# Thirteen result buffers, a later combine of the first half, and the positive part of the keys on VectorE

## The chip, the cores and the metric

The kernel runs on one core of a Trainium2 chip. Five engines work side by side, each on its own queue of instructions: TensorE (PE, with PEld for its weight loads), VectorE (DVE), ScalarE (ACT), GpSimd (POOL) and SyncE (SP, which here only issues transfers). They meet through semaphores. The metric is the device time of one execution in microseconds (us), the median of several runs.

## The reference

Two transformer layers in float32 over 2 x 2048 tokens of 128 channels. Layer 0 adds a Hyena attention (a projection, a convolution over three tokens, two long convolutions by FFT) and a mixture of 8 experts with 4 chosen, plus a shared expert. Layer 1, in which the whole change lies, is this:

```
xn = layernorm(x)
q, k = elu(xn @ wq + bq) + 1, elu(xn @ wk + bk) + 1;   v = xn @ wv + bv     # 16 heads of 8
kv = sum over n of k[n] v[n];   out = (q @ kv) / (q . sum k + 1e-6) @ wo + bo
scores[e] = norm(xn @ W_A[e]);   two best of 8 experts, weights by softmax
y[e] = W_down[e] (silu(W_B[e] W_A[e] xn) * W_up[e] xn)
x = x + out + sum over the two chosen experts of weight * y
```

elu(t) + 1 is computed as max(t, 0) + exp(-max(-t, 0)).

## The kernel before

The last two thirds of the time are one loop over 90 slots, written out by hand once for each engine; what an engine does in a slot, and in which order, is the order of the `if`s in its loop. An engine never passes an instruction that waits.

Slots 0 to 47 are eight chunks of 512 tokens, six slots each. In each slot TensorE makes one piece of the layer-0 experts (`gate0`, `up0_step`, `down0_step`), ScalarE its silu (L1174), VectorE the product (L1622) and GpSimd a weighting (L893). Behind that, at fixed distances from a chunk's end, comes layer 1 for that chunk: `due(slot, at)` gives the chunk whose end lies `at` slots back. Normalised tokens are turned, and then keys and values are multiplied in steps 7, 8, 10, 11 (`keys_values`), two tiles of 128 tokens to a bank; VectorE adds their bias in steps 9 and 12 (`key_bias`, L1605); ScalarE does all of `key_features` for both halves in step 13, and the exp of the queries (`query_exp`, L1148); VectorE adds both parts in step 14 (`key_sum`, L1693); TensorE sums keys times values in steps 15 and 16 (`key_value_sum`, L2079). `key_features` is, for each half,

```
nc.scalar.activation(KEX[:, j % 3], k, ACT.Relu, scale=-1.0).then_inc(k_neg, 1)        # L1091
act.wait_ge(k_neg, j + 1)
nc.scalar.activation(k, k, ACT.Relu)                                                    # L1093
nc.scalar.activation(KEX[:, j % 3], KEX[:, j % 3], ACT.Exp, scale=-1.0).then_inc(k_exp, 1)  # L1094
```

and exp needs another activation table than the silu, so a table load stands before the first exp of a block and before the silu after it. The steps of the last two chunks reach into the pair stage: steps 10 and 13 of chunk 6 are pair slots 0 and 3, those of chunk 7 are pair slots 6 and 9.

Slots 52 to 87 are the pair stage: pair slot i = slot - 52, 0 to 35. The tokens have been scattered by expert into rows in HBM (`scatter`, L863, one indirect transfer for 128 rows); there are at most 71 blocks of 128 rows, taken two at a time as 36 pairs. In slot i TensorE turns the rows of pair i+1 (L2099), makes the gate and up products of pair i (`gate_up`, three passes of split floats a block), turns the products of pair i-1 (L2128), and makes the down products of pair i-2 (L2143). Then one step of the attention of a chunk: denominators and numerators twice (L2163), turn (L2169), output product (L2174); this has a period of six slots for two interleaved halves. ScalarE copies rows_hi (L1101), takes the silu of pair i (L1108), copies the turned products of pair i-1 (L1115) and weights the results of pair i-2 into a result buffer (`result_rows`, L1125). VectorE computes rows_lo of pair i+1 (L1635), an attention step, the product of pair i (L1643) and its destinations (L1652 to L1657). The ranks of the last quarter of the router (L1499 to L1512) fall in pair slots 8 and 9; they free the roots on GpSimd (L850).

A result buffer holds one pair; there are YBUFS = 9, and `result_rows(i)` waits until the scatters of pair i - YBUFS have landed. GpSimd scatters the buffers to `result_rows` in HBM (`results`, L878). `shares()` lays down how many scatters GpSimd issues in each slot: PER_SLOT = 3, expert rows first, results with what is left, except that results which a buffer will need are forced. By it slot 16 has three rows and one forced result, slot 17 one row and two results, slots 18 to 33 three results each, slots 34 and 35 two each, and the rest follows behind the loop. GpSimd starts a slot's scatters when the gate products of that slot are done.

The combine brings results back in token order. SyncE's queue carries row loads (L729), and ahead of the row load of pair RESULTS_BEFORE = 34 the four loads of the first half of the tokens (`load_results(0)`, L741, 512 KB each), which wait until the scatters of pairs 0 to 23 (48 blocks) have landed. VectorE adds the first half from slot BACK_AT = 30 on, BACK_STEP = 2 tiles (one call of `combine`, L1665 and L1666) a slot. After the last scatter has landed come `load_results(1)`, the combine of the second half, and the stores.

Of the kernel before, what the change touches and what calls it, by code (L numbers as in the profile page):

```python
# [78 lines left out]
YBUFS = 9  # L79
# [11 lines left out]
BACK_AT, BACK_STEP = 30, 2  # L91
RESULTS_BEFORE = 34
# [9 lines left out]
COUNT_AT = (16, 16, 17, 14)  # L102
RANK_AT = ((13, 14, 15),) * 3 + ((12, 13, 13),)
# [19 lines left out]
def hyena_moe_program(nc, x, w_inT, conv_rows, peT, w1T, b1, w2b, fdec, fbias, w_outT, b_out,  # L123
# [8 lines left out]
    with ctx:  # L132
# [204 lines left out]
        YB = view(rW + 2560, YBUFS, 2, D)  # L337
        KTHF = view(rW + 2560 + YBUFS * 2 * D, RING, 2)
        DEST = view(rW + 2560 + YBUFS * 2 * D + 16, NP, 2).bitcast(I32)
        WROW = view(rW + 2560 + YBUFS * 2 * D + 16 + 2 * NP, RING, 2)  # L340
        KTHW = view(rW + 2560 + YBUFS * 2 * D + 32 + 2 * NP, RING, 2)
        assert 2560 + YBUFS * 2 * D + 48 + 2 * NP <= 5120 and 2 * RING <= 16
# [56 lines left out]
        first_x = sem("first_x")  # L399
        res_mm = sem("res_mm")  # L400
        res_out = sem("res_out")
        bout_in = sem("bout_in")
# [48 lines left out]
        up_hi = sem("up_hi")  # L451
        up_lo = sem("up_lo")
# [90 lines left out]

        def odd_due(s, at):

            c = due(s, at)
            return c // 2 if c is not None and c % 2 else None
# [47 lines left out]

        def last_use(end, n):

            return end - 1 - (end - 1 - n) % YBUFS
# [29 lines left out]
        def _(sp):  # L628
            sp.dma_start(X[:, 0:TPC, :], x[:, 0:TPC, :]).then_inc(first_x, 16)
# [29 lines left out]
            sp.wait_ge(st_wexp, 32)  # L659
# [7 lines left out]
            sp.wait_ge(pool_set, 2)  # L667
# [97 lines left out]
        def _(pool):  # L765
# [50 lines left out]
            for q in range(2 * NJ):  # L816
                if q == NJ:
# [5 lines left out]
                    ins.then_inc(bout_in, 1)  # L823
# [13 lines left out]
            def up_lo_part(n):  # L837

                if n == 0:
                    pool.wait_ge(up_hi, 1)  # L840
                es = slice(2 * n, 2 * n + 2)
                nc.gpsimd.tensor_tensor(out=GUL[:, es, F1W:2 * F1W], in0=UP1[:, es, :],
                                        in1=GUH[:, es, F1W:2 * F1W].bitcast(F32), op=ALU.subtract).then_inc(up_lo, 1)
# [28 lines left out]
            def results(m):  # L872

                for i, n in placed[stored[0]:stored[0] + m]:
                    if n == 0:
# [4 lines left out]
                        in_=YB[:, i % YBUFS, n, :], in_offset=None).then_inc(st_rows[i % YBUFS], 16)  # L880
                stored[0] += m

            for slot in range(SLOTS):
# [13 lines left out]
                if slot == UP_LO_AT + W_PARTS:  # L897
                    pool.wait_ge(split_hi, 3)
                    nc.gpsimd.tensor_tensor(out=WAL[:, :, :], in0=WA1, in1=WAH[:, :, :].bitcast(F32),
                                            op=ALU.subtract).then_inc(split_lo, 1)  # L900
                if slot == UP_LO_AT + W_PARTS + 1:
                    pool.wait_ge(split_hi, 4)
# [23 lines left out]
        def _(act):  # L926
# [124 lines left out]
            def prepare(slot):  # L1051

                if slot == UP_HI_AT:
                    act.wait_ge(ld_w1, N_W1)
                    nc.scalar.activation(GUH[:, :, F1W:2 * F1W], UP1, ACT.Copy).then_inc(up_hi, 1)
# [29 lines left out]
            def key_features(j):  # L1085
# [32 lines left out]
            def result_rows(i):  # L1118
# [5 lines left out]
                for n in range(blocks(i)):  # L1124
                    ins = nc.scalar.activation(YB[:, i % YBUFS, n, :], PS[6][:, P * n:P * (n + 1)], ACT.Copy,  # L1125
# [24 lines left out]
            for slot in range(SLOTS):  # L1150
# [53 lines left out]
        def _(dve):  # L1204
# [73 lines left out]
            def statistics(n):  # L1278
                first, last = PIECES[n]
                dve.wait_ge(ld_x[first // 8] if n else first_x, 16)  # L1280
# [149 lines left out]
            def residual(j):  # L1430

                dve.wait_ge(down_mm, N0 * (j + 1))
                if j == 0:
                    dve.wait_ge(bout_in, 1)
# [164 lines left out]
            def key_bias(j):  # L1599
                dve.wait_ge(kv_mm, j + 1)  # L1600
                if j == 0:
                    dve.wait_ge(pool_set, 3)
# [86 lines left out]
            def key_sum(j):  # L1689
# [3 lines left out]
                nc.vector.tensor_tensor(out=k, in0=k, in1=KEX[:, j % 3], op=ALU.add).then_inc(k_sum, 1)  # L1693
# [15 lines left out]
            for slot in range(SLOTS):  # L1709
# [6 lines left out]
                for h in range(2):  # L1716
                    c = due(slot, 9 + 3 * h)
                    if c is not None:
                        key_bias(2 * c + h)
# [15 lines left out]
                c = due(slot, 14)  # L1735
                if c is not None:
# [36 lines left out]
        def _(pe):  # L1773
# [242 lines left out]
            def turn_normed(c):  # L2016
# [11 lines left out]
            def keys_values(n):  # L2028
# [3 lines left out]
                if n == 0:  # L2032
                    pe.wait_ge(split_lo, 4)
# [15 lines left out]
            def expert_gates(n):  # L2049
                if n:  # L2050
                    pe.wait_ge(sq_in, n)
                else:
                    pe.wait_ge(split_lo, 3)
# [48 lines left out]
            def gate_up(i):  # L2102

                if i == 0:
# [3 lines left out]
                    pe.wait_ge(up_lo, W_PARTS)  # L2108
# [195 lines left out]
```

## Time and profile before

| | us |
|---|---|
| median of 3 runs | 621.71 (619.81 to 622.02) |
| profiled execution, its own time | 618.25 |
| its span, first to last instruction | 616.4 |
| PE busy | 557.1 (90%) |
| DVE busy | 433.7 (70%) |
| ACT busy | 314.3 (51%) |
| POOL busy | 297.4 (48%) |
| mean granted TensorE clock | 0.986 of full speed |

Busy time is a sum over the span and says little of a single stage. A row of a timeline gives the start, the duration, the engine, the line and the form of an instruction, and in brackets the time for which its engine stood idle before it and what ended that. "issue" is time in which the engine waited for nothing that the profile shows. The words "arena" and "banks" stand for all of the program's on-chip memory and for the accumulators of TensorE.

### The profile page before, as it was taken

To read this page: it belongs to the slowest core of one execution; us is meant where nothing else is said; L and a number is where in the kernel's file an instruction comes from. 1 tells how busy PE (TensorE), PEld (TensorE's weight loads), DVE (VectorE), ACT (ScalarE), POOL (GpSimd) and SP (SyncE) were. 2 spreads that over 40 slices of the span, in tenths; PEclk is the share of its full clock that TensorE was granted. 3 is DMA by queue.
4 is the path that set the end of the run, shared out by engine and by line. 5 is a ranking of instruction groups with operands and counts; after the bars stand their busy time and mean duration, and the time that the engine had idled before them with its cause. 6 is when DMAs were issued, how large, how long until landed. Compare 5 with 4: busy or idle time off the path is not lost.

```text
span 616.4 us, 10602 instructions
## 1 busy us (share of the span) xinstructions
PE 557.1 (90%) x3218; PEld 463.2 (75%) x3218; DVE 433.7 (70%) x1153; ACT 314.3 (51%) x625; POOL 297.4 (48%) x269
## 2 busy tenths in 40 slices
PE   6999999999989898999999999998889787999970
PEld 3879986576778676788888888876667676788870
DVE  6868998909931596335565998998878895566673
ACT  3560336764423444144456764765675854456550
POOL 4720030005561355147332446887735777577770
PEclk9999999999999999999999999999899999999995
DMA  6460031310040530323323223212322232323626
GB/s 206 155 256 18 2 136 27 77 44 2 1 138 0 178 118 1 94 70 89 88 81 85 56 79 94 86 42 85 92 57 64 61 103 84 88 83 89 228 82 230
DMA packets 48525, 54.94 MB, mean 89 GB/s; under 512 B 7045, under 2 KB 40390, under 8 KB 47415
## 3 DMA queue, kind: packets, MB, share of 16 engines
q1 hardware_dynamic: 43686, 42.99, 22.4%
q0 software_dynamic: 4320, 8.99, 4.2%
q10 hardware_dynamic: 466, 2.31, 1.7%
q8 instruction: 28, 0.46, 0.3%
q14 instruction: 25, 0.20, 0.1%
HBM read 36.22 MB, written 15.94 MB: 85 GB/s over the span
## 4 chain that ended last, share of the span: by engine, by line
PE 29%; DVE 11%; issue 8%; POOL 7%; ACT 7%; DMA 3%; SPq 0%; POOLq 0%; ACTq 0%; DVEq 0%
PE banks L1784 4%; PE banks L1786 3%; PE banks L1785 3%; PE banks L1992 3%; PE banks L2143 3%; PE banks L1906 2%; DMA arena<-result_rows 2%; POOL arena L893 2%; POOL result_rows L878 2%; PE banks L1898 2%; DMA result_rows<-arena 1%; PE banks L2128 1%; POOL expert_rows L863 1%; PE banks L1919 1%; PE banks L1920 1%
## 5 line engine op out<-in xcount | busy, mean ns | idle before, releaser
L878 POOL DMA_INDIRECT result_rows<-arena x71 | 69.1, 973 | 27.9 <-issue 16.6
L827 POOL TENSOR_TENSOR arena<-arena 128x512 f32<-128x512 f32 x32 | 40.8, 1274 | 86.2 <-DVE arena L1468 86.2
L863 POOL DMA_INDIRECT expert_rows<-arena x64 | 63.2, 988 | 30.9 <-issue 15.9
L893 POOL TENSOR_TENSOR arena<-arena 128x512 f32<-128x512 f32 x32 | 42.3, 1321 | 65.0 <-DVE arena L1622 64.9
L1622 DVE TENSOR_TENSOR arena<-banks,arena 128x512 f32<-128x512 f32 x48 | 33.0, 688 | 42.5 <-PE banks L1786 33.5
L1992 PEld LDWEIGHTS banks<-arena 128*128 128x128 f32 x384 | 48.8, 191 | 7.5 <-POOL arena L893 3.5
L1992 PE MATMUL banks<-arena 128*128 128x128 f32 x384 | 51.6, 277 | 2.5 <-POOL arena L893 1.5
L1898 PE MATMUL banks<-arena 128*128 128x512 f32 x96 | 50.5, 608 | 2.4 <-DVE arena L1468 1.1
L1906 PEld LDWEIGHTS banks<-arena 128*128 128x128 f32 x256 | 33.0, 191 | 19.0 <-POOL arena L827 14.4
L1174 ACT ACTIVATE arena<-banks 128x512 f32<-128x512 f32 x48 | 28.8, 599 | 36.2 <-PE banks L1786 31.7
L994 ACT ACTIVATE arena<-banks 128x512 f32<-128x512 f32 x48 | 28.7, 597 | 32.5 <-PE banks L1874 32.5
L2143 PE MATMUL banks<-arena 128*128 x284 | 38.4, 278 | 4.2 <-ACT arena L1125 3.8
L1023 ACT ACTIVATE arena<-banks 128x512 f32<-128x512 f32 x32 | 19.1, 597 | 39.4 <-PE banks L1906 39.4
L2143 PEld LDWEIGHTS banks<-arena 128*128 128x128 f32 x284 | 34.5, 192 | 5.8 <-issue 5.7
L1466 DVE TENSOR_TENSOR arena<-banks,arena 128x512 f32<-128x512 f32 x32 | 22.1, 692 | 23.7 <-PE banks L1898 22.1
L1906 PE MATMUL banks<-arena 128*128 128x128 f32 x256 | 34.4, 277 | 4.0 <-POOL arena L827 4.0
L1475 DVE TENSOR_TENSOR arena<-banks,arena 128x512 f32<-128x512 f32 x16 | 11.1, 692 | 34.5 <-PE banks L1920 34.5
L1784 PE MATMUL banks<-gate_up_weights_hi,rows_hi 128*128 x71 | 31.7, 446 | 3.6 <-DVE arena L1643 3.6
L1784 PE MATMUL banks<-projection_hi,xnt_hi 128*128 128x384 f32 (+1 forms) x92 | 33.4, 363 | 0.4 <-DVE xnt_lo L1274 0.4
L1643 DVE TENSOR_TENSOR arena<-banks,arena 128x512 f32<-128x512 f32 (+1 forms) x36 | 24.5, 679 | 13.0 <-ACT arena L1108 12.8
L1125 ACT ACTIVATE arena<-banks,arena 128x128 f32<-128x128 f32 x71 | 22.3, 365 | 21.4 <-DMA result_rows<-arena 12.2
L1082 ACT ACTIVATE arena<-banks 128x512 f32<-128x512 f32 x32 | 19.1, 596 | 26.0 <-PE banks L1786 14.1
(277 smaller groups left out, 1625.0 us busy)
## 6 DMA issues: line engine op xcount, KB each, us to landing
arena<-expert_weights SPq DMA_DIRECT2D x64, 128.0 KB, 3.3
arena<-expert_rows SPq DMA_DIRECT2D x71, 66.0 KB, 1.8
arena<-result_rows SPq DMA_DIRECT2D x8, 512.0 KB, 6.1
arena<-in_x SPq DMA_DIRECT2D x7, 512.0 KB, 7.1
arena<-in_dft_f SPq DMA_DIRECT2D x1, 2048.0 KB, 9.9
normed_hi<-xnt_hi SPq DMA_DIRECT2D x1, 2048.0 KB, 6.3
normed_lo<-xnt_lo SPq DMA_DIRECT2D x1, 2048.0 KB, 10.8
arena<-in_dft_i SPq DMA_DIRECT2D x1, 2048.0 KB, 7.7
```

Of the source, the lines that this page charges most:

```text
L827: nc.gpsimd.tensor_tensor(out=T1[:, q % 3, :], in0=T1[:, q % 3, :], in1=T2[:, q % 2, :], op=ALU.add).then_inc(y_in, 1)
L863: pool.indirect_dma_start(out=xrows, out_offset=bass.IndirectOffsetOnAxis(ap=SLOT[:, k, t:t + 1], axis=0), in_=XNF[:, t, :], in_offset=Non ...
L878: pool.indirect_dma_start(out=yrows, out_offset=bass.IndirectOffsetOnAxis(ap=DEST[:, i, n:n + 1], axis=0), in_=YB[:, i % YBUFS, n, :], in_ ...
L893: nc.gpsimd.tensor_tensor(out=AM0[slot % 2], in0=AM0[slot % 2], in1=WB0[:, m, :], op=ALU.mult).then_inc(weighted, 1)
L994: nc.scalar.activation(spread_rows(n % NI), bank(spread_bank(n % NI), 2, NGR, 4), ACT.Copy)\
L1174: nc.scalar.activation(SG0, PS[0], ACT.Silu).then_inc(silu_done, 1)
L1622: nc.vector.tensor_tensor(out=AM0[n % 2], in0=PS[1], in1=SG0, op=ALU.mult).then_inc(mult_done, 1)
L1784: mm(o, lh, rh, start=start, stop=False, skip_group_check=True)
L1898: mm(PS[2 + J % 2], TURNF, ZT[:, J % 2, :], start=True, stop=True).then_inc(d_mm, 1)
L1906: ins = mm(PS[6 + q % 2][:, P * n:P * (n + 1)], T1[:, q % 3, P * n:P * (n + 1)], TURNI, start=True, stop=True)
L1992: ins = mm(PS[2][:, D * t:D * (t + 1)], AM0[n % 2][:, P * t:P * (t + 1)], DW0[:, m, :], start=False, stop=(m == N0 - 1), skip_group_check= ...
L2143: ins = mm(PS[6][:, P * s:P * (s + 1)], AMT[:, i % 2, 2 * s + f, :], DN_FLAT[:, at], start=(f == 0), stop=(f == 1), skip_group_check=True)
```

## The change

The number of result buffers goes from 9 to 13. The first nine stay where they were; the other four lie in the region of the gated weights' staging, which is free by then. `shares()` and the waits follow from YBUFS, so the forced result of slot 16 goes, and slot 34 gets three results. The four loads of the first half stand ahead of the row load of pair 35 where they stood ahead of that of pair 34, and the combine of the first half starts in slot 32 with four tiles a slot where it started in slot 30 with two.

The positive part of the keys is no longer taken on ScalarE; VectorE's key sum takes it in the same instruction, max(k, 0) + exp part. The negative part of each half is taken one slot after its bias (steps 10 and 13), the exps of both halves stay in step 13.

Four semaphores make room for the four new buffers: `first_x` counts on `st_wexp`, `bout_in` on `pool_set`, `up_hi` on `split_hi` and `up_lo` on `split_lo`, with the numbers that are waited for raised accordingly. The steps of the key work are read from tables now, with the numbers that they had for all but the negative parts.

```diff
-YBUFS = 9
+YBUFS = 13
+Y_LOW = 9
-BACK_AT, BACK_STEP = 30, 2
-RESULTS_BEFORE = 34
+BACK_AT, BACK_STEP = 32, 4
+RESULTS_BEFORE = 35
+KEYS_AT = ((7, 8, 10, 11),) * NCH
+KEY_BIAS_AT = ((9, 12),) * NCH
+KEY_NEG_AT = ((10, 13),) * NCH
+KEY_EXP_AT = (13,) * NCH
+KEY_SUMMED_AT = (14,) * NCH
+KEY_VALUE_AT = ((15, 16),) * NCH
...
-        YB = view(rW + 2560, YBUFS, 2, D)
+        YB_LOW = view(rW + 2560, Y_LOW, 2, D)
+        YB_HIGH = view(rG + 2048, YBUFS - Y_LOW, 2, D)
...
+        def parts_due(s, table):
+
+            return [(c, n) for c in range(NCH) for n, at in enumerate(table[c]) if s == N0 * (c + 1) + at]
+        def result_buffer(i, n):
+
+            b = i % YBUFS
+            return YB_LOW[:, b, n, :] if b < Y_LOW else YB_HIGH[:, b - Y_LOW, n, :]
...
-            sp.dma_start(X[:, 0:TPC, :], x[:, 0:TPC, :]).then_inc(first_x, 16)
+            sp.dma_start(X[:, 0:TPC, :], x[:, 0:TPC, :]).then_inc(st_wexp, 16)
-            sp.wait_ge(st_wexp, 32)
+            sp.wait_ge(st_wexp, 48)
...
-                    pool.wait_ge(up_hi, 1)
+                    pool.wait_ge(split_hi, 3)
...
-            def key_features(j):
+            def key_negative(j):
                 act.wait_ge(kv_bias, j + 1)
                 if j >= 3:
                     act.wait_ge(kvs_mm, 2 * (j - 2))
                 k = KVS[:, j % 3, :, 0:P]
                 nc.scalar.activation(KEX[:, j % 3], k, ACT.Relu, scale=-1.0).then_inc(k_neg, 1)
+
+            def key_exp(j):
+
                 act.wait_ge(k_neg, j + 1)
-                nc.scalar.activation(k, k, ACT.Relu)
                 nc.scalar.activation(KEX[:, j % 3], KEX[:, j % 3], ACT.Exp, scale=-1.0).then_inc(k_exp, 1)
...
-                    ins = nc.scalar.activation(YB[:, i % YBUFS, n, :], PS[6][:, P * n:P * (n + 1)], ACT.Copy,
+                    ins = nc.scalar.activation(result_buffer(i, n), PS[6][:, P * n:P * (n + 1)], ACT.Copy,
...
-                c = due(slot, 13)
-                if c is not None:
-                    key_features(2 * c)
-                    key_features(2 * c + 1)
+                for c, h in parts_due(slot, KEY_NEG_AT):
+                    key_negative(2 * c + h)
+                for c in chunks_due(slot, KEY_EXP_AT):
+                    key_exp(2 * c)
+                    key_exp(2 * c + 1)
                     query_exp(c)
...
-                nc.vector.tensor_tensor(out=k, in0=k, in1=KEX[:, j % 3], op=ALU.add).then_inc(k_sum, 1)
+                nc.vector.scalar_tensor_tensor(out=k, in0=k, scalar=0.0, in1=KEX[:, j % 3], op0=ALU.max,
+                                               op1=ALU.add).then_inc(k_sum, 1)
...
-                    pe.wait_ge(up_lo, W_PARTS)
+                    pe.wait_ge(split_lo, 2 + W_PARTS)
```

## Rows read from the trace of the kernel before

**Rows 1.** Waits, 450 us on: who waited for whom, total, times, longest
```profile
ACT arena L1125 <- DMA result_rows<-arena: 12.2, 4, 5.3
```

**Rows 2.** ScalarE's timeline: start, us, line, form, [idle before, releaser]
```profile
521.25 0.63 ACT L1125 ACTIVATE arena<-banks,arena 128x128 f32<-128x128 f32 x2 [5.26 <-DMA result_rows<-arena]
...
598.45 0.37 ACT L1125 ACTIVATE arena<-banks,arena 128x128 f32<-128x128 f32 x1 [1.00 <-PE banks L2143]
```

**Rows 3.** GpSimd's timeline, pair stage
```profile
488.13 2.93 POOL L850 TENSOR_TENSOR arena<-arena 128x16 f32<-128x16 f32 x1 [1.74 <-DVE arena L1512]
...
491.50 1.19 POOL L878 DMA_INDIRECT result_rows<-arena  x1 [0.17 <-issue]
...
518.92 0.95 POOL L878 DMA_INDIRECT result_rows<-arena  x1 [0.30 <-issue]
...
596.32 1.17 POOL L878 DMA_INDIRECT result_rows<-arena  x1 [0.30 <-issue]
...
601.58 0.95 POOL L878 DMA_INDIRECT result_rows<-arena  x1 [0.30 <-issue]
```

**Rows 4.** TensorE's timeline: gate products of pairs 17,21,23,25,27,31,33
```profile
516.64 0.49 PE L1784 MATMUL banks<-gate_up_weights_hi,rows_hi 128*128 x1
...
537.75 0.48 PE L1784 MATMUL banks<-gate_up_weights_hi,rows_hi 128*128 x1
...
545.49 0.49 PE L1784 MATMUL banks<-gate_up_weights_hi,rows_hi 128*128 x1
...
553.29 0.48 PE L1784 MATMUL banks<-gate_up_weights_hi,rows_hi 128*128 x1
...
560.69 0.47 PE L1784 MATMUL banks<-gate_up_weights_hi,rows_hi 128*128 x1
...
576.08 0.48 PE L1784 MATMUL banks<-gate_up_weights_hi,rows_hi 128*128 x1
...
585.04 0.48 PE L1784 MATMUL banks<-gate_up_weights_hi,rows_hi 128*128 x1
```

**Rows 5.** The page's part 5: busy, mean ns, idle before, releaser
```profile
L878 POOL DMA_INDIRECT result_rows<-arena x71 | 69.1, 973 | 27.9 <-issue 16.6
```

**Rows 6.** ScalarE's timeline, pair slots 0, 3 and 4
```profile
444.08 0.38 ACT L1101 ACTIVATE rows_hi<-banks 128x256 fp32r<-128x256 f32 x1 [0.69 <-PE banks L2099]
...
453.93 0.41 ACT L1091 ACTIVATE arena<-arena 128x256 f32<-128x256 f32 x1
...
454.37 0.42 ACT L1093 ACTIVATE arena<-arena 128x256 f32<-128x256 f32 x1
...
461.17 0.60 ACT L1108 ACTIVATE arena<-banks 128x512 f32<-128x512 f32 x1
```

**Rows 7.** TensorE's timeline, pair slots 4, 5 and 10
```profile
458.72 0.63 PE L2128 MATMUL banks<-arena 128*128 128x128 f32 x4 [0.93 <-ACT arena L1115]
...
462.64 0.49 PE L1784 MATMUL banks<-gate_up_weights_hi,rows_hi 128*128 x1 [1.21 <-DVE arena L1643]
...
487.57 0.63 PE L2128 MATMUL banks<-arena 128*128 128x128 f32 x4 [2.15 <-ACT arena L1115]
```

**Rows 8.** VectorE's timeline, pair slot 30
```profile
577.77 0.43 DVE L1665 TENSOR_TENSOR arena<-arena 128x256 f32<-128x256 f32 x1 [1.50 <-DMA arena<-result_rows]
```

**Rows 9.** Line L741 alone: its loads of result rows
```profile
DMA to landing us min/median/max: 4.1/6.1/7.5
```

**Rows 10.** Windows: five engines' busy time, clock, DMA share, GB/s
```profile
300.00:400.00 100.00, 99.33 (x618) 86.49 (x617) 77.19 (x183) 64.14 (x121) 52.19 (x42) 1.00 0.28 79
...
435.00:440.00 5.00, 3.01 (x12) 2.19 (x13) 4.87 (x11) 1.79 (x5) 4.04 (x4) 0.86 0.28 74
...
585.00:590.00 5.00, 5.00 (x37) 4.60 (x36) 3.72 (x14) 2.86 (x7) 3.40 (x4) 1.00 0.17 56
```

**Rows 11.** VectorE's groups by form: busy, mean ns, idle before
```profile
L1396 DVE SCALAR_TENSOR_TENSOR arena<-arena 64x1024 f32<-64x1024 f32 x2 | 2.4, 1207 | 0.0
...
L1700 DVE TENSOR_TENSOR arena<-arena 128x512 f32<-128x512 f32 x8 | 5.5, 686 | 0.1
```

More of the change, by code:

```diff
@@ L336, in hyena_moe_program @@
         AMT = view(rI + 4096 + RING * 2 * RW, 2, 4, P)
-        YB = view(rW + 2560, YBUFS, 2, D)
[L338 to L342, printed above, removed]
+        k0 = rW + 2560 + Y_LOW * 2 * D
+        YB_LOW = view(rW + 2560, Y_LOW, 2, D)
+        YB_HIGH = view(rG + 2048, YBUFS - Y_LOW, 2, D)
+        KTHF = view(k0, RING, 2)
+        DEST = view(k0 + 16, NP, 2).bitcast(I32)
+        WROW = view(k0 + 16 + 2 * NP, RING, 2)
+        KTHW = view(k0 + 32 + 2 * NP, RING, 2)
+        assert 2560 + Y_LOW * 2 * D + 48 + 2 * NP <= 5120 and 2 * RING <= 16
+        assert (YBUFS - Y_LOW) * 2 * D <= 1024
         assert 4096 + RING * 2 * RW + 1024 <= 6528
@@ L542, in due, with chunks_due @@
             return c - 1 if rest == 0 and 0 <= c - 1 < NCH else None
+        def chunks_due(s, table):
+            return [c for c in range(NCH) if s == N0 * (c + 1) + table[c]]
+        def parts_due(s, table):
+            return [(c, n) for c in range(NCH) for n, at in enumerate(table[c]) if s == N0 * (c + 1) + at]
         def odd_due(s, at):
@@ L839, in up_lo_part @@
                 if n == 0:
-                    pool.wait_ge(up_hi, 1)
+                    pool.wait_ge(split_hi, 3)
                 es = slice(2 * n, 2 * n + 2)
                 nc.gpsimd.tensor_tensor(out=GUL[:, es, F1W:2 * F1W], in0=UP1[:, es, :],
-                                        in1=GUH[:, es, F1W:2 * F1W].bitcast(F32), op=ALU.subtract).then_inc(up_lo, 1)
+                                        in1=GUH[:, es, F1W:2 * F1W].bitcast(F32), op=ALU.subtract).then_inc(split_lo, 1)
             def root_of_norms(bt):
@@ L1279, in statistics @@
                 first, last = PIECES[n]
-                dve.wait_ge(ld_x[first // 8] if n else first_x, 16)
+                dve.wait_ge(ld_x[first // 8] if n else st_wexp, 16)
                 stats(first, last - first).then_inc(ln_var, 1)
@@ L1715, in _ @@
                     residual(c)
[L1716 to L1719, printed above, removed]
+                for c, h in parts_due(slot, KEY_BIAS_AT):
+                    key_bias(2 * c + h)
                 c = due(slot, 17)
@@ L1734, in _ @@
                     places_of(i)
-                c = due(slot, 14)
-                if c is not None:
+                for c in chunks_due(slot, KEY_SUMMED_AT):
                     key_sum(2 * c)
@@ L2188, in _ @@
                     fetch(i + 2)
-                for t, at in enumerate((7, 8, 10, 11)):
-                    c = due(slot, at)
-                    if c is not None:
-                        keys_values(TPC * c + t)
+                for c, t in parts_due(slot, KEYS_AT):
+                    keys_values(TPC * c + t)
                 if m == 0 and st < NCH:
@@ L2203, in _ @@
                     turn_normed(c)
-                for h in range(2):
-                    c = due(slot, 15 + h)
-                    if c is not None:
-                        key_value_sum(2 * c + h)
+                for c, h in parts_due(slot, KEY_VALUE_AT):
+                    key_value_sum(2 * c + h)
                 c = query_due(slot, 0)
```

26 lines of the change are left out of this document (11 added, 15 removed).

## The prediction

> **What bounds the kernel now.** I read the slices first, then the waits of the last 166 us, then each engine's timeline there, and the chain of waits last. The change touches three places, and only waits that end last there can pay.
>
> The first place is the middle of the pair stage. ScalarE waits 12.2 us in four waits for transfers into result_rows [rows 1]. In slot 16 it stands before the results of pair 14 until 521.25, for 5.26 us [rows 2]: with nine buffers pair 14 needs the buffer of pair 5, whose second block is the twelfth result scatter. GpSimd issues it at 518.92 [rows 3], because each slot has three scatters and slots 12 to 16 give theirs to expert rows. The three pairs after it wait in the same way and share the other 6.9 us. TensorE feels it: from the first gate product of pair 17 (516.64) to that of pair 21 (537.75) are 21.11 us, while the same four slots one attention period later (545.49 to 560.69) take 15.20 [rows 4]. VectorE's long waits for rows_hi there are the same hold, passed on through ScalarE's queue.
>
> The second place is the end. The last scatter is issued at 601.58 [rows 3]; its landing, four loads, the combine and the store fill the last 14.8 us of the span and stay as they are. Before it GpSimd is nearly solid: a scatter step is 0.973 us of work and 0.30 of issue, 1.275 us [rows 5], so three take 3.8 us of a 3.8 to 3.9 us slot.
>
> The third is the key work. In pair slots 3 and 9 ScalarE runs back to back from the silu over two negative parts, two positive parts, table load, exps to the turned copy, a second table load and the next silu. TensorE waits 0.93 us for the turned copy and 1.21 us for the product behind the silu in slot 4, 2.15 us in slot 10, behind the block of slot 9 [rows 6, 7].
>
> **Part 1: thirteen buffers.** Nothing is added but addresses. Working the order of scatters through: 11 result scatters are out by slot 14, 13 by slot 17, then three a slot. Pair i needs 2i-24 of them before its slot i+2; pair 17 needs 10 and has 11, pair 18 needs 12 and has 13, and from there supply grows by three and demand by two. So all four waits go, and the buffers hold no one again. Slots 17 to 20 fall to the 15.20 us of their later twins: TensorE gains 5.9 us. What is late next is TensorE itself; bounds 5 (the second waits keep part) and 6.5.
>
> The forced result scatter of slot 16 also goes; slot 34 gets three scatters where it had two. By TensorE's clock the last scatter then comes one step, 1.3 us, later.
>
> **Part 2: first half combined from slot 32.** Now the combine of slot 30 waits 1.50 us for the load [rows 8], and TensorE's slots 31 and 32 take 8.96 us (576.08 to 585.04) against 7.40 for their twins (553.29 to 560.69): 1.6 us to gain [rows 4]. The load needs result scatter 48, which moves from first to second of slot 29; issued some 8 us earlier than now all the same, at about 565, it lands near 567. The four loads are issued then, and the first lands 4.1 to 7.5 us later [rows 9], at 571 to 575. VectorE would reach the first combine at about 575. Chunk 0 is then there or short by tenths. Row load 34 moves ahead of the four loads, row load 35 stays behind them and is not needed before 579.
>
> Per slot VectorE now does four operations of 0.43 us instead of two, 0.86 us more. It was busy 3.72 of 5 us at 585 [rows 10], so a 3.9 us slot has 1.0 us free: it just fits in slots 32 and 33. Slot 34 has an attention sum too and overruns by about 0.6 us, which holds the product of the last pair by 1 to 2 us. That pair's results are ready at 598.82 and its scatter starts at 601.58 [rows 2, 3]: 2.8 us of cover, and 1.3 more by the added step. I take nothing for it; uncovered it would cost 0.6 to 2 us. Row by row, then, +1.6 gain, bounds 0 and 1.6.
>
> **Part 3: keys.** ScalarE loses 16 positive parts of 0.43 us, and one negative part of each chunk moves to the slot of step 10. In the block of step 13 that leaves one negative part instead of four relus: 3 x 0.43 = 1.3 us shorter, less about 0.1 where the next engine is not ready. The moved part stands behind a silu in pair slots 0 and 6; in slot 0 a wait of 0.69 us for TensorE covers its 0.43 us [rows 6], in slot 6 a longer one. The bias sum that it waits for is one slot older and stands ahead of that slot's product, so nothing queued behind it (row split, squares, turned copy) waits for VectorE. It costs nothing; uncovered, 0.43 us twice. With nothing in its way the silu of slot 4 goes from 461.17 to 460.0 and the gate product behind it from 462.64 to 461.4: 1.2 us [rows 6, 7]. Behind slot 9's block the same 1.2 us. In the six chunks before the pair stage I take nothing: TensorE is busy 99.33 us of 300 to 400 [rows 10], and from about 365 VectorE is solid too, which has its rank and table work between these blocks; bounds 0 and 2 us.
>
> The key sum on VectorE becomes a three-operand operation on 128x256. That form took 1207 ns for 1024 elements a partition, and the two-input sum 686 ns for 512 [rows 11]: both about 1.02 ns an element beyond a start of 0.15. The price of the swap is 0, bounds -0.1 and +0.1 us each, off the path in most chunks.
>
> The shared semaphores count the same events in the same queue's order; I find no wait that ends later. Price 0.
>
> **The sum.** TensorE reaches pair 34 earlier by 5.9 + 1.6 + 1.2 + 1.2 = 9.9 us; less the added step, its own schedule would bring the last scatter 8.6 us earlier. But GpSimd has its own floor. Its last unbroken run starts at 491.50, behind the roots of 488.13 [rows 3], which wait for VectorE's ranks: these move by slot 3's 1.2 us but not by slot 9's. From there 82 scatters (16 rows, 66 results) follow, 81 steps of 1.275 = 103.3 us, where the trace has 110.1. So GpSimd can gain 6.8 + 1.2 = 8.0 us, and that is the smaller. The two schedules run within a microsecond of each other, so small waits stay: I take 7.6. The profiled execution took 618.25 us (span 616.4 and 1.85 around it) and would take 610.7; it lies 3.5 us below the median of 621.71, so I subtract from the median: **614.1 us**.
>
> A page of the Trainium skill speaks against part 2. Some scatters are longer than the rest, 1.17 us at 596.32 where 0.96 is usual, with a combine running beside them [rows 3]. "SBUF — State Buffer", section "SBUF: two separate sides", says that GpSimd cannot write its descriptors while a VectorE operation holds the port pair that both share. Taken at its harshest (the page counts an operation with two inputs as a holder only against some GpSimd operations), a fully held scatter would cost 0.85 us for each of eight combines, 6.8 us in either kernel; the row shows 0.2, and the mean step above has it in it. What the page would change is only that the combines now all fall where GpSimd has no idle time: 8 x 0.2 less what is paid already, under 1 us, a rival below.
>
> **Rivals.** (a) The keys pay nothing, because VectorE's work between them ends as late as now. For it: VectorE is busy 70% and more around both blocks. Against: in both, the wait of VectorE's product is for the silu. TensorE's schedule then gives 5.9 + 1.6 - 1.3 = 6.2 us: 615.5. (b) GpSimd takes more back: combines four to a slot lengthen scatters where it has no idle time, a step of 1.30 instead of 1.275. 81 x 0.025 = 2 us: 616.1, and with (a) 617.5. (c) The keys also pay before the pair stage, two chunks at 1 us, and shift everything, ranks included: 612. (d) Slower: the loads of the first half land late. VectorE then stands in slot 32 before a combine, with the row split of pair 34 queued behind it, TensorE idles, and all 16 tiles are crowded into the last slots. After waits of TensorE the granted clock fell once, to a share of 0.86 of 435 to 440 [rows 10]; at the lower level, 1.2 GHz, the remaining slots would take 2 to 3 us more each. It decides from about 10 us of lateness on (2.4 + 7.6): 624 or more. Against it: the longest landing is 7.5 us. (e) The buffers are not what ends the wait: if scatters were late by more than four pairs, the wait would only move back. The count above excludes it unless row scatters slip; then about 3 us stay, 617.
>
> **Chances.** Forecast (612.8 to 615) 0.42; (a) 0.17; (b) 0.13; (c) 0.14; (d) 0.03; (e) 0.04; some other loss that leaves it within 3 us, 0.07. The range 610.5 to 617.8 leaves out (d), the far end of (c) and most of the last. A measurement of this kernel can tell 0.5%, 3.1 us, from no change: faster 0.88, same 0.09, slower 0.03.
>
> **What would show it.** Right: no wait of ScalarE's result copy for result_rows; TensorE's slots 17 to 20 in 15 to 16 us; GpSimd's scatters from slot 10 on almost unbroken, with few waits for TensorE; no wait of the combine at slot 32 over 0.5 us; key blocks shorter by 1.2 us, with the pair-4 silu earlier by as much against the gate product before it; the last 14.8 us unchanged. Wrong: a wait for a transfer before a result copy, a wait of over 1 us at slot 32, three-operand sums above 0.5 us, or a last scatter that is not 6 to 9 us earlier.

## The result and the profile after

The changed kernel took 614.45 us in the median of 14 runs (612.50 to 619.46), the kernel before 620.57 us in 14 runs beside it (617.72 to 624.41). The ratio is 0.991 with a 95% interval of 0.9886 to 0.9935: 6.1 us faster. The profiled execution took 618.34 us (span 616.5), no less than the 618.25 us of the one before, so the two traces can't be compared end to end. This is why. Most runs of the changed kernel fall in two groups, near 613.5 us at a mean granted clock of about 0.984 and near 618 us at 0.976 or less, and the profiled one is of the second. What it lost, it lost ahead of the pair stage: its window of 150 to 300 us has a granted clock of 0.97 where the kernel before has 1.00, and the pair stage starts 4.2 us later (silu of pair 0 at 447.01, before 442.79; two profiles of the first group, taken later, have it at 442.26 and 442.25). I therefore measure from that silu on.

ScalarE's waits of the changed kernel for anything in the pair stage: the group for `result_rows` of [rows 1] is gone. What is left of transfers is this (waits of all engines from 440 us on: who, for whom, total, times, longest):

```profile
DVE arena L1687 <- DMA arena<-result_rows: 11.8, 1, 11.8
PEld banks L2119 <- DMA arena<-expert_rows: 2.2, 1, 2.2
PE banks L2119 <- DMA arena<-expert_rows: 2.0, 1, 2.0
```

The first is the end of the kernel, as before. The other two are new. TensorE's timeline, gate products of pairs 17, 18, 19, 21, 23, 27, 31 and 33, and what precedes that of pair 19 (it answers to [rows 4]):

```profile
518.53 0.49 PE L1804 MATMUL banks<-gate_up_weights_hi,rows_hi 128*128 x1
...
522.76 0.47 PE L1804 MATMUL banks<-gate_up_weights_hi,rows_hi 128*128 x1
...
528.21 0.50 PE L2119 MATMUL banks<-arena 128*128 128x128 f32 x2 [2.01 <-DMA arena<-expert_rows]
528.43 0.79 PE L1804 MATMUL banks<-gate_up_weights_hi,rows_hi 128*128 x1
529.02 0.63 PE L1805 MATMUL banks<-gate_up_weights_lo,rows_hi 128*128 x1
...
537.32 0.48 PE L1804 MATMUL banks<-gate_up_weights_hi,rows_hi 128*128 x1
...
545.06 0.49 PE L1804 MATMUL banks<-gate_up_weights_hi,rows_hi 128*128 x1
...
560.30 0.48 PE L1804 MATMUL banks<-gate_up_weights_hi,rows_hi 128*128 x1
...
575.66 0.48 PE L1804 MATMUL banks<-gate_up_weights_hi,rows_hi 128*128 x1
...
583.09 0.48 PE L1804 MATMUL banks<-gate_up_weights_hi,rows_hi 128*128 x1
```

Pair 17 to 21 takes 18.79 us where it took 21.11; the twins, pair 23 to 27, take 15.24. Pair 17 to 18 has come down from 7.52 to 4.23 us, but pair 18 to 19 takes 5.67: TensorE stands 2.01 us before it turns the rows of pair 20. Pair 31 to 33 takes 7.43 us, before 8.96.

GpSimd's timeline, against [rows 3]: the roots, the start of the unbroken run, the last three expert rows, the first idle time, the last scatter:

```profile
491.16 2.93 POOL L869 TENSOR_TENSOR arena<-arena 128x16 f32<-128x16 f32 x1 [1.74 <-DVE arena L1534]
...
494.78 1.04 POOL L897 DMA_INDIRECT result_rows<-arena  x1 [0.17 <-issue]
...
519.24 0.96 POOL L882 DMA_INDIRECT expert_rows<-arena  x1 [0.30 <-issue]
520.50 0.96 POOL L882 DMA_INDIRECT expert_rows<-arena  x1 [0.30 <-issue]
521.76 0.96 POOL L882 DMA_INDIRECT expert_rows<-arena  x1 [0.31 <-issue]
...
531.63 0.95 POOL L897 DMA_INDIRECT result_rows<-arena  x1 [2.58 <-PE banks L1806]
...
601.46 0.96 POOL L897 DMA_INDIRECT result_rows<-arena  x1 [0.30 <-issue]
```

Pair 20 is the first whose rows can contain tokens of the last quarter, so its load waits for the 64th expert row. That one is issued at 521.76 and lands some 2.3 us later; then the load runs; TensorE gets its rows at 528.21. While TensorE stands, GpSimd has no gate product to start slot 19 on, and it idles too, 2.58 us at 531.63. From roots to last scatter are 110.30 us; before it was 113.45. From the last scatter to the end of the span are 15.0 us, before 14.8.

The key block of pair slot 3 on ScalarE, silu to silu ([rows 6] has the silu at its end before):

```profile
457.65 0.60 ACT L1129 ACTIVATE arena<-banks 128x512 f32<-128x512 f32 x1 [0.70 <-PE banks L1806]
458.15 0.41 ACT L1110 ACTIVATE arena<-arena 128x256 f32<-128x256 f32 x1
458.57 1.28 ACT L1115 ACT_TABLE_LOAD   x1
459.87 0.72 ACT L1115 ACTIVATE arena<-arena 128x256 f32<-128x256 f32 x2
...
464.19 0.60 ACT L1129 ACTIVATE arena<-banks 128x512 f32<-128x512 f32 x1
```

6.54 us, before 7.74; the block of slot 9 went from 7.27 to 6.07. The three-operand key sum (line L1715 alone: ns of one, min/median/max) costs what the sum cost, 420 ns in the median against 422, but for one of 16, one of the first two, which takes 1.49 us beside a product of GpSimd, where the plain sum took 1.05 in the same place:

```profile
L1715 DVE SCALAR_TENSOR_TENSOR arena<-arena x16: 413/420/1491, 325.6 to 493.5; 128x256 f32<-128x256 f32 x16
```

### The profile page after: what moved, and what is told of

The parts are those of the page before. It is cut to its first block, busy times and chain, and to the rows that moved or that the text cites. A ratio compares the mean times of both kernels' runs of the same rounds, so it can differ in the third digit from the quotient of the medians.

```text
span 616.5 us, 10590 instructions
## 1 busy us (share of the span) xinstructions
PE 558.6 (91%) x3218; PEld 465.3 (75%) x3218; DVE 434.0 (70%) x1153; ACT 309.3 (50%) x609; POOL 298.1 (48%) x269
## 4 chain that ended last, share of the span: by engine, by line
PE 36%; DVE 11%; POOL 6%; issue 5%; ACT 4%; DMA 2%; SPq 0%; POOLq 0%; ACTq 0%; DVEq 0%
PE banks L1804 5%; PE banks L1806 5%; PE banks L1805 5%; PE banks L2012 4%; PE banks L2163 3%; POOL expert_rows L882 3%; PE banks L1926 2%; PE banks L1918 2%; PE banks L2148 2%; PE banks L1939 1%; PE banks L1940 1%; DMA arena<-result_rows 1%; DVE arena L1665 1%; POOL arena L912 1%; PE banks L1907 1%
## 5 line engine op out<-in xcount | busy, mean ns | idle before, releaser
L1665 DVE TENSOR_TENSOR arena<-banks,arena 128x512 f32<-128x512 f32 (+1 forms) x36 | 24.5, 680 | 15.1 <-ACT arena L1129 15.0
L1129 ACT ACTIVATE arena<-banks 128x512 f32<-128x512 f32 (+1 forms) x36 | 21.3, 593 | 26.2 <-PE banks L1806 26.1
```

## The experiments

The kernels ran on three chips, each with its own runs of the kernel before. Ratios are to the kernel before on the same chip. A ratio is not the quotient of the two medians in its row (e5 and e6 have medians 3.9 us apart and ratios of 0.9906 and 0.9912), and it is the ratio with its interval that compares two kernels.

### On a chip with a slower pair stage

The changed kernel once more (e1), and

```diff
 e2_keys_only: nine buffers and the combine of before, only the key work changed
-YBUFS = 13
-Y_LOW = 9
+YBUFS = 9
+Y_LOW = 8
-BACK_AT, BACK_STEP = 32, 4
-RESULTS_BEFORE = 35
+BACK_AT, BACK_STEP = 30, 2
+RESULTS_BEFORE = 34

 e3_old_keys: thirteen buffers and the late combine, key work of before
-                nc.vector.scalar_tensor_tensor(out=k, in0=k, scalar=0.0, in1=KEX[:, j % 3], op0=ALU.max,
-                                               op1=ALU.add).then_inc(k_sum, 1)
+                nc.vector.tensor_tensor(out=k, in0=k, in1=KEX[:, j % 3], op=ALU.add).then_inc(k_sum, 1)
 (and key_features on ScalarE again)

 e4_four_scatters_early: as changed, four scatter steps in pair slots 3 to 8
-                n = min(PER_SLOT, known - rows)
+                per = PER_SLOT + (slot < PAIR0 + 9)
+                n = min(per, known - rows)
...
-                m = max(min(PER_SLOT - n, made - results), late - results, 0)
+                m = max(min(per - n, made - results), late - results, 0)
```

> The changed kernel again, as the measure for the others on this chip. Theory A (a new wait: the rows of pair 20 are loaded only when the last expert-row scatter has landed, and with the buffer waits gone this load is the last to arrive, in every execution): about 614.5 us, TensorE waits 1.5 to 3 us before it turns the rows of pair 20, with the clock at half for some products behind it. Theory B (that wait came only from the low clock upstream in the one profiled execution): about 614.5 us, and in an execution whose span is near 612 no such wait.

> Nine buffers and the combine from slot 30 as before, keys as changed. Theory A: the 1.2 us won behind slot 3's block reach the end, the 1.2 us behind slot 9's block don't, since the buffer wait of slot 16 is set by GpSimd's scatters, which start behind the roots and not behind the silu: 1.2 us faster than before. Theory B (gains add up): 2.4 us faster.

> Thirteen buffers and the later combine, keys as before. Theory A: slot 9's key gain is swallowed in the changed kernel too, by the row load of pair 20, so without the key change the time is 1.2 us above the changed kernel, 5 us below before; the wait before the turn of pair 20's rows is 1.2 us shorter than in the changed kernel. Theory B: 2.4 us above the changed kernel.

> The changed kernel with four scatters instead of three in pair slots 3 to 8, so that six more results are out by slot 10 and GpSimd's run behind the roots holds fewer. It does not move the last row scatter relative to the roots (slots 10 to 12 keep their three scatters each), so theory A keeps the wait before pair 20, 1.5 to 3 us, and gains only at the end, where GpSimd is no longer behind: the last scatter follows TensorE's last result, 1.5 to 3 us faster than the changed kernel. Theory C (GpSimd's floor of 1.275 us a scatter was the bound, and the row load only a detail): 5 us or more faster. Theory D (the fourth scatter delays the roots of slot 10): not faster.

| | median us | ratio | 95% interval |
|---|---|---|---|
| before | 638.22 | | |
| e1 changed | 636.45 | 0.9988 | 0.9952 to 1.0024 |
| e2 keys alone | 637.97 | 0.9974 | 0.9939 to 1.001 |
| e3 old keys | 639.41 | 1.0012 | 0.9974 to 1.0051 |
| e4 four scatters early | 642.42 | 1.0036 | 0.9997 to 1.0075 |

This chip is some 17 us slower for the kernel before and 22 us for the changed one, and here the change gains nothing that can be told. Up to the pair stage there is nothing to see: e1 has its silu of pair 0 at 442.44, where the changed kernel has it elsewhere too (442.26 in e5). Behind it most slots take 4.5 us and more where they took 3.8. ScalarE's waits of e1 from 450 to 600 us show them as waits that nothing in the trace ends ("remote"), and one of them in its timeline:

```profile
ACT rows_hi L1122 <- remote: 22.2, 9, 3.0
...
ACT arena L1146 <- remote: 9.5, 3, 4.0
```

```profile
546.88 0.38 ACT L1122 ACTIVATE rows_hi<-banks 128x256 fp32r<-128x256 f32 x1 [3.04 <-remote]
```

The matmuls and scatters are all in this trace; the scatters of results take 977 ns in the mean, before 973, and the matmuls theirs wherever the clock is whole. The granted clock of 450 to 600 us is 0.95, against 0.98 in e5 below, which by my estimate (0.03 of 150 us) is some 5 us of the 22. The rest lies between the instructions, and I can't say what it is.

No ratio there rules a part of the change in or out. The sizes forecast for e1 to e3 could not be met on this chip: TensorE's wait before the turn of pair 20's rows is there in e1 and e3, but with 0.70 and 0.60 us and not 1.5 to 3; e3 is 0.24%, 1.5 us, over e1 by the ratios, where 1.2 and 2.4 had been the theories, and the intervals are wider than that. Four scatters in slots 3 to 8 do not help, the outcome of theory D. Its cause isn't shown: the roots come 56.1 us after the silu of pair 0 (e1: 44.9), but GpSimd itself stands 3.92 us before them, waiting for VectorE's ranks, behind slots in which ScalarE has two waits without a releaser, 8.3 us together. The parts are told apart on the other chips.

### The parts, and the new wait

The control (e5), the keys alone again (e7, the edit of e2), and

```diff
 e6_two_results_less: as changed, but
-                m = max(min(PER_SLOT - n, made - results), late - results, 0)
+                m = max(min(PER_SLOT - n, made - results) - 2 * (slot == PAIR0 + 11), late - results, 0)

 e8_buffers_alone: thirteen buffers, key work of before (as e3), and
-BACK_AT, BACK_STEP = 32, 4
-RESULTS_BEFORE = 35
+BACK_AT, BACK_STEP = 30, 2
+RESULTS_BEFORE = 34
```

> The changed kernel once more, the control of this call. Theory A (the change's gain of 6 us is the gain wherever the pair slots run at some 3.8 us each): ratio to the kernel before 0.991, as when it was first timed. Rival B (the gain depends on the chip; on the chip of the first four experiments, whose pair slots took 4.6 us, it was 0.1%): ratio anywhere from 0.99 to 1.00, nearer to 1 where the time before is nearer to 638 us.

> In slot 11 GpSimd scatters two results fewer, so that the 64th expert row, for which the row load of pair 20 waits, is scattered 2.55 us sooner (two steps of 0.96 + 0.30 us); the two results are scattered later. Theory A (the wait of 2.0 us before the turned rows of pair 20, and TensorE's half clock after it, are the price that the thirteen buffers laid bare): the wait at pair 20 is under 0.3 us, slot 18 to 19 takes about 3.5 us in place of 6.97, and the time is 2 to 3.4 us under the changed kernel (the waits of GpSimd behind slot 19, 2.58 + 0.84 us, are all that its steps can gain). Rival B (GpSimd's steps set the end, and what is put off in slot 11 comes back at the end): within 1 us of the changed kernel, the slot short but the end as late. Rival C (other waits, for buffers or for the late results, come in): slower than the changed kernel by 1 to 2.5 us.

> Nine buffers and the combine of before; only the key work changed. Theory A (the two shorter slots, 7.74 to 6.54 and 7.27 to 6.07 us, come through to the end): 2.4 us under the kernel before, ratio 0.996. Rival B (GpSimd waits for the buffers in the same places anyway, so that sooner keys only lengthen the wait of slot 16 to 17): ratio 0.999 to 1.001, and ScalarE's wait for a result buffer 2.4 us longer than the 5.3 us of before.

> Old key work, thirteen buffers, the combine at slot 30 in steps of two slots and the results before slot 34 as before. Theory A (the buffers take 4.2 us off slot 16 to 17 and the row load of pair 20 gives 3.5 of it back in slot 18 to 19, less here because rows and turn both come later): ratio 0.997 to 0.999. Rival B (without the shorter keys the wait for the row load is not met, as GpSimd's row scatters do not depend on the keys): ratio 0.993 to 0.995, no wait at pair 20.

Then, on a third chip, the control (e9) and three more:

```diff
 e10_early_combine: as changed, but
-BACK_AT, BACK_STEP = 32, 4
-RESULTS_BEFORE = 35
+BACK_AT, BACK_STEP = 30, 2
+RESULTS_BEFORE = 34

 e11_four_late: as changed, but
-                n = min(PER_SLOT, known - rows)
-                behind = RESULT_LAG if slot < PAIR0 + NP else 0
+                per = PER_SLOT + (slot >= PAIR0 + 20)
+                n = min(per, known - rows)
+                behind = RESULT_LAG if slot < PAIR0 + 30 else 0
...
-                m = max(min(PER_SLOT - n, made - results), late - results, 0)
+                m = max(min(per - n, made - results), late - results, 0)

 e12_rows_and_four: as e11 with per = PER_SLOT + (slot >= PAIR0 + 12), and the "- 2 * (slot == PAIR0 + 11)" of e6
```

> The changed kernel, control of this call. Theory A (the gain of 6 us holds on a chip whose time before is about 620 us): ratio to before 0.991. Rival B (on a chip at some 638 us it is lost again): ratio 0.998 to 1.000.

> The changed kernel with the first half combined from pair slot 30 in steps of two slots and the results before slot 34 only, as before: thirteen buffers and the new key work stay. Theory A (in slots 31 and 32 VectorE's combine makes TensorE wait, and the late combine takes 1.5 us off these two while the added scatter step at the end gives back up to 1.3): 0 to 1.5 us over the changed kernel. Rival B (with GpSimd ahead or level, the loads of the first half are waited for at slot 31, as the slot of 5.73 us of the kernel with the buffers alone suggests, where the changed kernel takes 3.5): 1.5 to 2.5 us over the changed kernel, and a VectorE wait for the first half's rows in that slot.

> The changed kernel with four scatter steps in a slot from slot 20 on where results are there, and the results of the last six slots without the lag of one pair. Theory A (GpSimd's steps set the end; behind slot 19 it waits for TensorE's slots for 2.1 us beyond the 0.30 of each step, since it has only three steps for a slot of 4.3 us, and closing these waits shows at the end): the last scatter starts 2.1 us sooner after the first silu than in the changed kernel (154.3 us in the profile of e5) and the time is 2.1 us under it. Rival B (the end is ScalarE's last result copy, not GpSimd): the last scatter right behind that copy, a gain under 1 us. Rival C (scatters earlier collide with row loads or with the first half's loads): no gain or a loss, with a slot longer by over 0.5 us behind slot 20.

> As the kernel with four scatter steps from slot 20 on, but four steps already from slot 12 on, and two results fewer in slot 11, so that the expert rows for pair 20 go out sooner. Theory A (both waits of the changed kernel, TensorE's at pair 20 and GpSimd's behind it, cost time one behind the other): slot 18 to 19 under 5 us, no wait of GpSimd over 0.6 us behind slot 11, and the time 2.5 to 3.5 us under the changed kernel. Rival B (GpSimd's row of steps from the roots on, 103.0 us without a wait, is the floor): 2.5 us under the changed kernel at most, no better than 0.5 us against the kernel with four steps from slot 20 on. Rival C (four row scatters in the short slots 12 and 13 hold up the key work or the row loads): slower than the kernel with four steps from slot 20 on by over 0.5 us.

The last three columns are from each kernel's profiled execution: "stage" is the span less the start of the silu of pair 0 (before: 616.4 - 442.79), "GpSimd" the start of the last scatter less that of the roots, and the last the longest wait of TensorE before it turns the rows of pair 20. They leave the clock's early loss out, which moves the medians. One kernel's stage is not the same each time: the changed kernel's is 169.5, 169.3 and 168.4 us in three profiles, so a difference of 1 us between two stages says nothing.

| | median us | ratio (95%) | stage | GpSimd | pair 20 |
|---|---|---|---|---|---|
| before, chip 2 / chip 3 | 620.67 / 621.47 | | 173.6 | 113.5 | none |
| e5 changed | 613.86 | 0.9906 (0.9868 to 0.9943) | 169.3 | 110.2 | 1.9 |
| e6 two results less | 617.75 | 0.9912 (0.9871 to 0.9954) | 169.6 | 110.4 | 1.3 |
| e7 keys alone | 620.25 | 0.9987 (0.9963 to 1.001) | 174.2 | 115.2 | none |
| e8 buffers alone | 619.35 | 0.9972 (0.9939 to 1.0005) | 171.7 | 111.5 | 1.0 |
| e9 changed | 616.48 | 0.9919 (0.9885 to 0.9953) | 168.4 | 109.3 | 2.1 |
| e10 early combine | 619.48 | 0.9941 (0.9912 to 0.9969) | 172.2 | 112.9 | 2.2 |
| e11 four late | 613.78 | 0.9869 (0.9834 to 0.9904) | 168.2 | 109.0 | 2.1 |
| e12 rows and four | 613.73 | 0.9865 (0.9825 to 0.9905) | 165.6 | 106.4 | none |

The row of before is one profile, the one shown ahead of the prediction; I have none of it from chips 2 and 3.

**The gain is there again** (e5, e9): 0.9906 and 0.9919, theory A of both.

**Keys alone pay nothing that can be told.** e7 has its blocks at 6.53 and 6.07 us, 1.2 shorter each, and yet a ratio of 0.9987, whose interval leaves out the 0.996 of theory A, and the longest stage of all. ScalarE waits for the same buffers, in its timeline:

```profile
525.50 0.63 ACT L1146 ACTIVATE arena<-banks,arena 128x128 f32<-128x128 f32 x2 [6.22 <-DMA result_rows<-arena]
...
529.78 0.63 ACT L1146 ACTIVATE arena<-banks,arena 128x128 f32<-128x128 f32 x2 [1.92 <-DMA result_rows<-arena]
...
537.15 0.63 ACT L1146 ACTIVATE arena<-banks,arena 128x128 f32<-128x128 f32 x2 [4.37 <-DMA result_rows<-arena]
```

Rival B holds in substance, but not in size: the first of these waits was 5.26 us before [rows 2] and is 1.0 us longer, not 2.4, and the sum, 12.5, is hardly more than the 12.2 of [rows 1]. TensorE's clock takes another 1.7 us: behind its own wait of 3.99 us it goes on at half clock, and the down products and the output products, 526.38 to 529.85, take 3.47 us where the changed kernel's take 1.79 (520.83 to 522.62). Windows of e7:

```profile
526.00:530.00 4.00, 3.62 (x17) 3.62 (x18) 1.64 (x7) 2.08 (x6) 1.62 (x2) 0.57 0.22 63
```

This profile is of the slowest of e7's twelve runs, so its stage counts for less than the ratio.

With thirteen buffers the keys' worth is not settled. e10 differs from e8 by the new keys alone. Its stage is 0.5 us longer, since TensorE waits at pair 20 for what two shorter blocks save, but its ratio, on another chip, is 0.3% lower, with overlapping intervals. Slot 18 to 19 takes 7.21 us in e10, whose clock fell behind the wait, and 4.72 in e8, whose did not. TensorE's timeline, of e10 and of e8:

```profile
529.62 0.54 PE L2119 MATMUL banks<-arena 128*128 128x128 f32 x2 [2.24 <-DMA arena<-expert_rows]
```

```profile
527.22 0.44 PE L2114 MATMUL banks<-arena 128*128 128x128 f32 x2 [1.05 <-DMA arena<-expert_rows]
```

**Buffers alone** (e8) shorten the stage by 1.9 us, the ratio within theory A (its interval reaches to 1.0005). The wait at pair 20 is met even without the new keys, so B falls.

**The late combine is worth 1.4 us by the ratios and more by the profiles.** e10's stage is 2.7 to 3.8 us longer than those of the changed kernel; the ratios are 0.9941 and 0.9919 (e9, the same chip), which is 1.4 us, with overlapping intervals. VectorE's timeline of e10 shows the wait of [rows 8] doubled, since TensorE now comes to slot 30 sooner than the rows do:

```profile
580.30 0.43 DVE L1687 TENSOR_TENSOR arena<-arena 128x256 f32<-128x256 f32 x1 [3.06 <-DMA arena<-result_rows]
```

By the profiles that is rival B of that run, with a larger price than I gave it; the 1.4 us of the ratios lie within theory A.

**Two results less in slot 11** (e6) falls out as its rival B said: slot 18 to 19 came down to 4.93 us (the changed kernel's takes 6.97, 6.05 and 5.81 in its three profiles), and GpSimd's way from the roots to its last scatter stayed at 110.4. The 64th row came 1.0 us sooner, not 2.55 (73.8 us after the silu of pair 0 against 74.8), since GpSimd, with fewer steps in slot 11, had to wait for the gate products of slots 15 and 16. GpSimd's timeline of e6:

```profile
512.42 0.95 POOL L882 DMA_INDIRECT expert_rows<-arena  x1 [1.36 <-PE banks L1806]
...
516.75 0.96 POOL L882 DMA_INDIRECT expert_rows<-arena  x1 [0.85 <-PE banks L1806]
```

The idle time changed place and not size: what counts is each microsecond in which GpSimd stands anywhere between the roots and the end. The table says the same. The stage less GpSimd's time is 60.1 or 60.2 us with the old keys and 59.0 to 59.3 with the new, whose roots come sooner; all other differences between stages are in GpSimd's column.

**Four steps in late slots** (e11) removed GpSimd's idle time behind slot 19 but for one of 0.43 us. By the medians it is 2.7 us under e9 (ratios 0.9869 and 0.9919, intervals overlapping), but the profiles show less, a stage of 168.2 us against 168.4 and 169.3. Between theory A and rival B it is not settled.

**Rows sooner and four steps** (e12) is the kernel in which GpSimd has no idle time. Its timeline, roots, start of its run and last scatter, with at most 0.32 us between one scatter and the next from the second line to the third:

```profile
491.02 2.93 POOL L870 TENSOR_TENSOR arena<-arena 128x16 f32<-128x16 f32 x1 [1.73 <-DVE arena L1535]
...
494.63 1.03 POOL L898 DMA_INDIRECT result_rows<-arena  x1 [0.17 <-issue]
...
597.44 0.96 POOL L898 DMA_INDIRECT result_rows<-arena  x1 [0.30 <-issue]
```

102.8 us for the run, against the 103.3 that the prediction worked out as its floor. Slot 18 to 19 takes 3.44 us; pair 17 to 21 by the silus takes 4.24 + 3.44 + 3.60 + 3.86 = 15.1 us, the 15.2 of the twins. The stage is 2.8 to 3.9 us under the changed kernel's and 8.0 under before's, and by the medians e12 is 2.75 us under e9, as theory A had it. The medians of e11 and e12 are the same, though (613.78 and 613.73), as rival B had it, while their stages differ by 2.6 us. The quickest run of e12 took 610.07 us, that of e11 611.94, of e9 612.38. I take both as faster than before and, by the profiles, e12 as the better one; the medians of six runs each don't show that.

## Why the prediction was right, and where it was not

The time was forecast at 614.1 us and is 614.45; the gain was forecast at 7.6 us and is 6.1. That the time is hit to 0.4 us is luck: the gain was put 1.5 us too high and the base 1.1 us too high, and the two errors offset each other. I subtracted from 621.71, the median of three runs, and that of fourteen, these three among them, is 620.57. By the traces the stage gained 4.1, 4.3 and 5.2 us (173.6 less 169.5, 169.3 and 168.4). The single profile of before was quicker than its median by 2.3 us, and where its usual run spends these isn't in a trace. Two signs of the forecast failed: TensorE's slots 17 to 20 took 18.8 us and not 15 to 16, and the last scatter comes 4.3 us earlier against the silu of pair 0 (154.45 us behind it, before 158.79) and not 6 to 9.

**Thirteen buffers: the waits went, the gain of 5.9 us did not come whole.** All four waits for `result_rows` are gone, and pair 17 to 21 gained 2.3 us. The step that failed is "what is late next is TensorE itself". Late next was the row load of pair 20, behind the 64th expert row. Under the old hold TensorE came to it at 527.9, when it was in; that the trace of before showed no wait there said only that something else was later. I had worked through the order of the result scatters and not that of the expert rows in the same slots, and "turns the rows of pair i+1" puts that need a slot ahead of pair 20's own. e12 shows the size: with this wait away too, the four slots take the forecast 15.2. Of the 3.6 us that are missing, 2.0 are the wait itself and 1.6 the granted clock: from the first gate product of pair 19 to the down products behind it (528.43 to 531.94) are 3.51 us, for pair 20 (533.46 to 535.36) 1.90. Windows of the changed kernel (columns as in [rows 10]):

```profile
522.00:526.00 4.00, 4.00 (x31) 3.69 (x30) 2.05 (x8) 2.27 (x6) 3.09 (x4) 1.00 0.17 53
526.00:528.00 2.00, 0.21 (x2) 0.00 (x0) 0.31 (x4) 0.38 (x2) 1.48 (x2) 1.00 0.47 131
528.00:532.00 4.00, 3.79 (x13) 3.09 (x14) 1.30 (x4) 0.98 (x2) 1.33 (x2) 0.57 0.31 88
```

Behind the idle time the clock is granted at 0.57 over 4 us, so mostly at 1.2 GHz: a pass takes 0.63 us where it takes 0.40. The clock's part is not there each time: in e9 the wait is 2.13 us and the clock stays whole, and slot 18 to 19 takes 5.81 us and not 6.97.

**The late combine: right.** 8.96 to 7.43 us, 1.5 gained of 1.6; no wait at slot 32. The overrun of slot 34, put at 0.6 us, is there: the gate product of pair 35 follows that of pair 34 by 3.80 us, before 3.17. Rival (d) did not occur.

**The keys: right in place; their worth at the end is not shown.** Each block is 1.20 us shorter. But e7 shows nothing of it at the end, and e10 against e8 leaves it open; the changed kernel with the old keys ran only on the slower chip (e3). Rival (a) had such an outcome for another reason (VectorE); what the runs show is that GpSimd's schedule decides. Its roots moved by 1.2 us against the silu of pair 0 (45.34 to 44.15), as predicted. In e7 GpSimd's time from there to its last scatter grew by 1.7 us (113.5 to 115.2) and took that back; e12, without idle time, has the 1.2 us in its 8.0. Ahead of the pair stage the keys give little: its first silu comes at 442.25 to 442.70 us in e1, e5, e9 and e11, before at 442.79, so rival (c), 2 us, did not occur.

**The added scatter step: right.** Last silu to end of span 22.99 us before, 24.42 now: 1.4 for 1.3. e8, which has the step and the combine of before, takes 24.33.

**GpSimd's floor: right, and the best term of the sum.** It allowed 8.0 us, and e12's stage has gained 8.0. The changed kernel didn't come within the 0.4 us of it that I took: "the two schedules run within a microsecond of each other" was judged without the wait at pair 20. That wait holds GpSimd too, because each slot's scatters wait for a gate product. Its run took 106.7 us (494.78 to 601.46) against the floor of 103.3, and 2.58 - 0.30 = 2.3 of the 3.4 are the idle time at 531.63.

Rival (b), a step of 1.30 us, did not occur. The price that the prediction worked out from the Trainium skill's page "SBUF — State Buffer", section "SBUF: two separate sides", for the combines beside GpSimd does not show in the mean: of 71 result scatters it is 971 ns, before 973.

```profile
L897 POOL DMA_INDIRECT result_rows<-arena x71 | 69.0, 971 | 25.0 <-issue 17.8
```

Rival (e) occurred in its size, "about 3 us stay", but not in its mechanism: the buffers were what ended those waits, and another transfer took their place.

## What to carry to other kernels

Before crediting the removal of a wait, list every transfer that is due inside the stretch that closes up, with the slot in which its first reader stands, and date each against the new schedule. That a trace shows no wait for one of them proves nothing while an engine is being held by another. Where one engine must issue a fixed number of steps, count steps times duration first; any other saving counts only as far as it lets that engine start sooner or stand less.

## What the runs showed of the hardware

- On one of the chips the kernel before took 17 us more and the changed one 22, the latter all in the last third (stage of e1 191.5 us, e5 169.3), where the trace shows waits without a releaser. A gain of 1% on the other chips was 0.1% there.
- How long TensorE stands idle does not by itself tell whether its clock falls. Before the turn of pair 20 it stood 2.01 us in the changed kernel and 2.05 in e11 and went on at half clock (0.63 us a pass); it stood 1.93 us in e5 and fell to it 1.2 us later; it stood 2.13 us in e9, and 2.88 us in the kernel before, and kept its full clock. After 1.25 us in e6 and 1.05 in e8 it kept it too. TensorE's timeline, of e9 and of the kernel before:

```profile
523.46 0.44 PE L2119 MATMUL banks<-arena 128*128 128x128 f32 x2 [2.13 <-DMA arena<-expert_rows]
523.68 0.49 PE L1804 MATMUL banks<-gate_up_weights_hi,rows_hi 128*128 x1
524.01 0.40 PE L1805 MATMUL banks<-gate_up_weights_lo,rows_hi 128*128 x1
```

```profile
522.14 1.15 PE L2143 MATMUL banks<-arena 128*128 x8 [2.88 <-ACT arena L1125]
```
